# A transformer block on one core: who scales and copies the first tiles, eighteen extra turns of the identity, and the order in which the convolution's first operands are made

## What is computed

```python
def _layernorm(x, axis=-1, eps=1e-05):
    m = jnp.mean(x, axis=axis, keepdims=True)
    v = jnp.var(x, axis=axis, keepdims=True)
    return (x - m) / jnp.sqrt(v + eps)
...
        x = lax.conv_general_dilated(inputs, conv_w, window_strides=(1,), padding='SAME', dimension_numbers=('NWC', 'WIO', 'NWC')) + conv_b
        q, k, v = jnp.split(x, 3, axis=-1)
...
        scores = jnp.where(causal, scores, NEG_INF)
        p = jax.nn.softmax(scores, axis=-1)
        o = jnp.einsum('bhqk,bkhe->bqhe', p, vh)
        o = jnp.einsum('bqhe,hed->bqd', o, wo) + bo
        o = o.reshape(N, L, W_)
        return o @ proj_w + proj_b
...
    x = x + _L0_attn_ref(_layernorm(x, axis=-1), ...)
    x = x + _L0_ffn_ref(_layernorm(x, axis=-1), ...)
```

## Time and profile before

| | |
|---|---|
| median of 3 runs | 822.52 us (820.74 to 822.99) |
| the profiled execution | 821.56 us, of which the span of instructions is 819.7 us |
| TensorE busy, share of the span | 790.8 us, 96% |
| VectorE busy | 463.6 us, 57% |
| ScalarE busy | 407.5 us, 50% |
| GpSimd busy | 196.7 us, 24% |
| mean granted clock of TensorE | 0.997 |

### The profile page before, as it was taken

One profiled execution on the slowest core, in us unless ns is written; L12 is line 12 of the kernel. 1 busy time (PEld: TensorE's weight loads), 2 busy tenths in 40 slices (PEclk: granted clock), 3 DMA queues, 4 the chain that ended last, 5 costly groups with the idle time before them and its releaser, 6 DMA issues.

```text
span 819.7 us, 14315 instructions
## 1 busy us (share of the span) xinstructions
PE 790.8 (96%) x5248; PEld 704.1 (86%) x5248; DVE 463.6 (57%) x1359; ACT 407.5 (50%) x1085; POOL 196.7 (24%) x184
## 2 busy tenths in 40 slices
PE   3899999999999999999999999999999999999997
PEld 3798887777778788888888888888789999999996
DVE  6899966778877643333333434444684444444441
ACT  5953342344335997676868686867750111111010
POOL 2300103223230434252525253432300010100000
PEclk9999999999999999999999999999999999999999
DMA  8745833533436221211252411202143231313201
GB/s 333 254 123 173 261 121 114 205 120 110 155 141 239 88 106 39 105 39 72 94 235 84 114 62 49 90 1 104 67 139 108 75 104 52 103 52 103 73 31 52
DMA packets 41369, 94.03 MB, mean 115 GB/s; under 512 B 9299, under 2 KB 18387, under 8 KB 40020
## 3 DMA queue, kind: packets, MB, share of 16 engines
q1 hardware_dynamic: 38996, 84.73, 31.0%
q0 software_dynamic: 2304, 8.39, 2.5%
HBM read 66.63 MB, written 26.08 MB: 113 GB/s over the span
## 4 chain that ended last, share of the span: by engine, by line
PE 78%; DVE 11%; ACT 5%; issue 3%; POOL 2%; DMA 0%; DVEq 0%; ACTq 0%; POOLq 0%
PE net_psum L63 15%; PE net_psum L65 15%; PE net_psum L64 15%; PE net_psum L1208 10%; PE net_psum L1275 5%; PE net_psum L1294 4%; PE net_psum L1286 4%; POOL raw L478 2%; PE net_psum L1192 2%; PE net_psum L1326 2%; PE net_psum L1327 2%; PE net_psum L1340 2%; PE net_psum L1328 2%; DVE raw L891 1%; DVE raw L892 1%
## 5 line engine op out<-in xcount | busy, mean ns | idle before, releaser
L63 PE MATMUL net_psum<-fw_hi,xT_hi 128*128 128x354 f32 (+1 forms) x384 | 126.0, 328 | 0.4 <-DVE fw_lo L1059 0.4
L65 PE MATMUL net_psum<-fw_hi,xT_lo 128*128 128x354 f32 (+1 forms) x384 | 124.4, 324 | 0.0
L64 PE MATMUL net_psum<-fw_lo,xT_hi 128*128 128x354 f32 (+1 forms) x384 | 124.2, 324 | 0.0
L495 POOL TENSOR_TENSOR pr<-pr,rrec 128x512 f32<-128x512 f32 x64 | 66.7, 1042 | 219.9 <-DVE rrec L958 213.5
L631 ACT ACTIVATE pr<-pr,negmax 128x128 f32<-128x128 f32 x256 | 99.2, 392 | 12.3 <-DVE negmax L965 12.3
L1208 PE MATMUL net_psum<-ua,wa 128*128 128x256 f32 x384 | 85.5, 385 | 2.3 <-DVE ua L849 2.3
L1208 PEld LDWEIGHTS net_psum<-ua,wa 128*128 128x128 f32 x384 | 73.7, 193 | 12.7 <-issue 2.6
L965 DVE CUSTOM_DVE_ANT_0 pr<-net_psum,mask 128x128 f32<-128x128 f32 x256 | 58.8, 287 | 42.6 <-PE net_psum L1275 42.5
L63 PE MATMUL net_psum<-x_hi,w_hi 128*128 128x512 f32 x192 | 77.1, 401 | 3.2 <-DVE w_lo L898 3.0
L63 PE MATMUL net_psum<-c_hi,wqk_hi 128*128 128x256 f32 x256 | 76.8, 300 | 0.4 <-ACT kf L640 0.4
L478 POOL TENSOR_TENSOR raw<-raw 128x512 f32<-128x512 f32 x24 | 37.3, 1557 | 164.5 <-ACT raw L578 164.5
(11 more groups left out here) (174 smaller groups left out, 1824.0 us busy)
## 6 DMA issues: line engine op xcount, KB each, us to landing
wa<-in_conv_w SPq DMA_DIRECT2D x24, 512.0 KB, 4.1
raw<-in_conv_w SPq DMA_DIRECT2D x24, 384.0 KB, 3.4
xn<-in_x SPq DMA_DIRECT2D x16, 512.0 KB, 10.1
xr<-in_x SPq DMA_DIRECT2D x8, 1024.0 KB, 5.0
x_scratch<-xr SPq DMA_DIRECT2D x8, 1024.0 KB, 4.0
x1t<-x_scratch SPq DMA_DIRECT2D x16, 512.0 KB, 4.0
out<-y POOLq DMA_DIRECT2D x16, 512.0 KB, 5.0
c_raw<-c_scratch SPq DMA_DIRECT2D x7, 768.0 KB, 4.7
```

Of the source, the lines that this page charges most:

```text
L63: pe.matmul(out, w_hi, x_hi, start=first, stop=False)
L64: pe.matmul(out, w_hi, x_lo, start=False, stop=False)
L65: return pe.matmul(out, w_lo, x_hi, start=False, stop=last)
L495: pool.tensor_tensor(pr[:, jj % 4], pr[:, jj % 4], rrec[:, jj % 4].unsqueeze(2).to_broadcast([P, UN, P]), ALU.mult).then_inc(s["p_ready"], 1)
```

## The change

In the front three things change. ScalarE and VectorE trade work: VectorE scales tiles 5, 6 and 7 of sequence 0 (before: 2, 6, 7), copies the whole turned tile 6 and half of tile 7 (before: half of tile 7), and brings the statistics of the first tile to an end before it begins those of the second. TensorE gets 18 products of the identity with itself (`FILL`), behind the turns of sequence 0 and ahead of the first unit; their result is not used. At the start of the split units, steps are moved: on ScalarE `high_weight(1)`, `pre_scale(2)` and the last `high_input` go ahead of the last `first_out`; on VectorE `low_weight(0)` goes behind the last `inputs` and `low_input(6)`.

The change's own description also names a reordering from attention to dense in the tail. No line of the diff is in that part, and the instructions of GpSimd and SyncE stand in the same order in both kernels.

```diff
-    DVE_SCALES = (2, LT - 2, LT - 1)
+    DVE_SCALES = (LT - 3, LT - 2, LT - 1)
+    ACT_OUT = LT - 1
...
+    FILL = 18
...
             def conv_slot(k):
-                if k + 1 < NK:
+                if 0 < k < NK - 1:
                     high_weight(k + 1)
-                if k == 0:
-                    high_input(DC - 1)
                 if k % NP4 == 0 and k:
                     evacuate(k // NP4 - 1)
-                if k + 2 < NK:
+                if 0 < k < NK - 2:
                     pre_scale(k + 2)
...
-            for j in range(LT):
+            for j in range(LT - 1):
                 if j not in DVE_SCALES:
                     scale(0, j)
                 if j:
...
             high_weight(0)
             first_out(4)
             high_input(6)
+            high_weight(1)
+            pre_scale(2)
+            high_input(7)
             first_out(5)
...
-                for j in range(lo, LT):
+                for h in range(2):
+                    half_statistics(n, lo, h)
+                moments(n, lo)
+                add_eps(n, lo)
+                for j in range(lo + 1, LT):
                     half_statistics(n, j, 0)
-                    if j > lo:
+                    if j > lo + 1:
                         moments(n, j - 1)
+                    if j != lo + 2:
+                        finish(n, max(j - 2, lo))
+                    half_statistics(n, j, 1)
                     if j > lo + 1:
-                        finish(n, j - 2)
-                    half_statistics(n, j, 1)
-                    if j > lo:
                         add_eps(n, j - 1)
...
-                if k == 0:
-                    low_input(DC - 1)
...
+            dve.wait_ge(s["transposed"], LT - 1)
+            planes = stepped(xT, 32 * (LT - 2), (N * ROW, DC), (QUADS + 1, 4), (1, 32))
+            dve.tensor_copy(planes, turned(0, LT - 2).rearrange("p b (c t k) -> p (b c) k t", k=4, t=32)).then_inc(s["xT_dve"], 1)
...
-                if c == DC - 2:
-                    low_weight(0)
+            low_weight(0)
+            low_input(DC - 1)
...
             for j in range(LT):
                 transpose_tile(0, j)
+            pe.wait_ge(s["xT_ready"], LT // 2 + 1)
+            for i in range(FILL):
+
+                pe.transpose(turned(0, LT // 2)[:, 0, i % 4 * P:(i % 4 + 1) * P], ident[:], ident[:])
             for a in range(NA):
```

More of the change, by code:

```diff
@@ L1113, in _ @@
             dve.tensor_copy(planes, turned(0, LT - 1)[:, 1].rearrange("p (c t k) -> p c k t", k=4, t=32)).then_inc(s["xT_dve"], 1)
-            dve.wait_ge(s["xT_ready"], LT)
+            dve.wait_ge(s["xT_ready"], ACT_OUT)
+            dve.wait_ge(s["xT_dve"], 1)
             first_inputs(0, 0, 1)
             first_inputs(0, 1, 1)
-            dve.wait_ge(s["xT_dve"], 1)
+            dve.wait_ge(s["xT_dve"], 2)
             for c in range(2, DC, 2):
@@ L1123, in _ @@
                 inputs_of(0, c, c + 1)
-            dve.wait_ge(s["xT_ready"], N * LT)
+            dve.wait_ge(s["xT_ready"], ACT_OUT + LT)
             for c in range(0, DC, 2):
@@ L1189, in transpose_tile @@
                 normalised(n, j)
-                wait(pe, s["xT_ready"], j - 3 if n == 0 else LT + j - 1)
+                wait(pe, s["xT_ready"], j - 3 if n == 0 else ACT_OUT + j - 1)
                 for c in range(DC):
@@ L1200, in first_unit @@
                     if d == 0:
-                        pe.wait_ge(s["xT_ready"], LT)
-                        pe.wait_ge(s["xT_dve"], 1)
+                        pe.wait_ge(s["xT_ready"], ACT_OUT)
+                        pe.wait_ge(s["xT_dve"], 2)
                     wait(pe, s["a_evac"], 2 * (d - 1))
```

## The result

| | before | after |
|---|---|---|
| median of five runs each, side by side | 821.51 us (820.74 to 822.99) | 817.11 us (816.88 to 817.28) |
| the profiled execution | 821.56 us, span 819.7 | 817.15 us, span 815.4 |
| TensorE busy in it | 790.8 us | 791.7 us |
| mean granted clock in it | 0.997 | 0.999 |

The ratio is 0.9944 (95% interval 0.9932 to 0.9956): 4.4 us faster, inside the range and 0.8 under the predicted time. The two profiled executions lie 4.41 apart.

What follows compares the result with a forecast made beforehand. TensorE, busy 96% of the span, was taken as the bound. Gains 1.0 + 1.9 - 0.85 + 0.67 + 0.98 + 0.5 = 4.2 us gave 817.4 or 818.3, middle 817.9; range 816.0 to 820.3.

Steps and rivals of the forecast that it cites:

- The front: Sequence 0 ahead of the first unit: that unit starts at 24.85 instead of 25.83, gain 1.0 us (0.5 to 1.3).
- The two new costs on VectorE: In the front: uncovered aggregate of tile 0, 0.3 us, and the whole copy of tile 6, 1.3 us.
- ScalarE's last scale: In the front: now tile 4, expected near 17.3 to 18.5 us; TensorE's last four tiles were reckoned from 18.5.
- The late rise of the clock: Rival, turns of sequence 0: low clock lasts through their small pauses; 821.5, or 819.5 to 820.5 if risen before 25; chance 0.10.
- The clock: First 48 unit products: the 18 products close the empty stretch and the clock stays at 1.00, gain 1.9 us or 0.
- main case: Whole kernel: all terms hold, gain 4.2 us, time 816.3 to 819.2; chance 0.62.
- the clock falls all the same: Rival, first units: 1.9 lost but unit 0's 0.85 wait goes; gain 3.1, 818.5 to 819.4 us; chance 0.16.
- The split units: First split units: new wait of 0.85 us at unit 0, against waits of 0.67, 0.98 and 0.5 of 0.57 won.
- the overlap: Ahead of the split units: GpSimd's `mix(2)` runs inside VectorE's `inputs(7)`, costing VectorE 1.1 us.
- The half of 0.96 added for the median: Final time: median of runs stood 0.96 above the profiled execution, so the middle of 817.4 and 818.3 was taken.
- Gain given back later: Rival, behind the changed places: for instance a transfer due by the clock takes it back; 821.6 to 822.5 us; chance 0.04.
- VectorE no earlier: Rival, long stretch before the split units: VectorE gains nothing, unit 0 waits 2.85; 819.4 to 820.3 us; chance 0.08.

Runs made afterwards that it cites:

- the order alone: The kernel before with only the moved steps on ScalarE and VectorE at the first split units: 819.07 us, ratio 0.9971 (12 runs).

## Why the prediction was right, and where it was off

**The bound** was read rightly: TensorE is busy 97% of the span, and what was won at the two places is still won at the end.

**The front** was worth 0.79 by the profiles, not 1.0. The two new costs on VectorE were 0.34 and 1.23, as the working had them (0.3 and 1.3). What it had too early is ScalarE's last scale: TensorE turns the last four tiles from 18.80, not from 18.5, and VectorE waited 0.30 for tile 6. Another 0.17 is the start of the first statistics, 5.83 instead of 5.66 in this pair of executions. The quicker copy, and 2.15 instead of 2.24 from the half copy to the first unit, gave part of this back. The late rise of the clock, a rival, did happen in a small way: 8 turns took 1.67 at 16.75, where 16 in 1.75 is the full rate. It was over before the last four tiles.

**The clock.** The products took 0.109 us each, as predicted, ended 0.48 ahead of the first unit, and the clock stayed at 1.00: 1.69 won in the 48 products, against 1.9 predicted. The working set three times 3.46 against 12.29, but 48 in a row at the higher level take 10.60, not 10.38. The page of the Trainium skill that the prediction weighed, "TensorE: Matmul & The Clock Gate", Part 4 (PE-mode transpose), says that a transpose does not count as PE work in the same way and that the full rate does not engage for it. By it the products would hold nothing. The traces disagree: the clock read 1.00 behind them in all six profiles, and was low in six of eight without them.

The step that failed is the one ahead of it: "Now the first 48 unit products took 12.29 ... so 48 would take 10.38: 1.9 us were lost after the empty stretch". This took one execution's low stretch for a property of the kernel. By the mean clocks five of 50 executions have none, and 18 have two. Alone the products are worth 0.84 in the medians: by the mean clocks a part of the executions keeps a low stretch that they don't reach. In the changed kernel they are worth 0.86 in the medians (817.97 to 817.11), or 0.95 against the executions with a low stretch, because there a TensorE that is not slowed meets unit 0's wait; with that wait gone it is 1.62. The working foresaw this second mechanism: its main case and its rival "the clock falls all the same", 4.2 and 3.1, put 1.1 there.

**The split units.** VectorE began `inputs(7)` at 106.29 (106.1 predicted), lost 1.06 to the overlap (1.1), and TensorE waited 0.68 for unit 0 (0.85). The recorded waits 0.67, 0.98 and 0.57 went, and the last two stayed (0.84 in all, 0.8 predicted). The terms were mis-sized by one thing: a wait costs more than its record. The last first units and unit 0's first product, before and, as the third row, the last first units in the change:

```profile
107.11 10.52 PE L1208 MATMUL net_psum<-ua,wa 128*128 128x256 f32 x48
117.28 0.58 PE L63 MATMUL net_psum<-x_hi,w_hi 128*128 128x512 f32 x1
...
112.83 2.32 PE L1217 MATMUL net_psum<-ua,wa 128*128 128x256 f32 x10
```

Before, unit 0's first product began at 117.28, that is 0.35 ahead of the recorded end of the last first unit; after, it waits for 0.68 from that end, so the new wait costs 1.03. Taking it away was worth 0.95 in the medians. Likewise units 1 and 2 gain 0.92 and 1.24 where 0.67 and 0.98 were written in the rows. A short hold leaves no record at all, as at unit 0 in the order alone (0.28). Unit 7 gains 0.44 (0.5 predicted): it starts 5.89 behind unit 6, where 5.60 is usual, at 155.42, right behind the end of its `low_weight` at 155.37.

**The sum.** 0.79 + 1.69 - 1.03 + 0.92 + 1.24 + 0.44 is 4.05, a further 0.09 lies between units 2 and 3, and the rest of the 4.41 is spread over the 650 us behind. The working had 4.2. The front and the clock brought 0.42 less than it had and the split units 0.27 more, so that the sum came this close is partly luck. Taken from the profiled execution it gave 817.4, 0.3 from the result. The half of 0.96 added for the median was an error: the 822.52 of three runs was an accident of which low stretches they had, and the median over the 50 executions is 821.62, close to the profiled execution's 821.56.

**"Gain given back later"** didn't happen. **"VectorE no earlier"** fell with the 106.29.

## What to carry to other kernels

Before a term of a sum is taken from a stretch at a low clock, look at the clock in several executions: whether it falls behind a short empty stretch can differ from one execution to the next, and filling the stretch then buys a steadier time as much as a shorter one. Work of GpSimd that nobody waits for yet should not be released while VectorE makes an operand that TensorE waits for; here putting one `pre_scale` behind a copy was worth 0.95 us. A recorded wait of TensorE is a lower bound: here three of them cost 0.25 to 0.35 us more than their rows say. Two gains that end in the same wait are not independent: time how much lateness the next wait takes up before pricing either.

## What the runs showed of the hardware

- The granted clock fell behind an empty stretch of 2.4 us in six of eight profiled executions without the products, and stayed at 1.00 in two. What decides it was not found: the clock had risen at 14.7 to 18.1 us where it fell, and at 14.6 and 17.5 where it didn't. A second fall, among the last turns, was seen in one execution, behind pauses of 1.36, 0.94 and 0.99 us; pauses of 1.20, 0.94 and 0.98 in one other and of 1.32, 0.94 and 0.99 in a third, with the products, had none behind them. A mean clock of 0.995 or less, which went with two low stretches, stands in 21 of 62 executions with the turns of before (the kernel before and the order alone) and in one of 24 with the new turns and no products. So the changed front, whose pauses are 0.21 and 0.38 at 16.75 and 18.80, seems to be rid of that second fall; this is argued from the mean clocks, no profile shows it by itself.
- In the overlaps of GpSimd and VectorE seen here the one that began later paid. In the changed kernel `mix(2)` began at 110.34, VectorE's piece at 110.68, and the piece took 1.06 longer; with 36 products the overlap fell on the `low_input` at 111.52 behind a `mix(2)` that began at 111.34, and that took 3.37 instead of 2.28. With `pre_scale(2)` put behind the copy, `low_weight(1)` began at 116.59, 0.11 ahead of `mix(2)`; it kept its 1.22, and `mix(2)` took 2.26, ending 1.15 behind it. (The 1.72 of `mix` in the next two units is no undisturbed time either: each began inside a `low_weight` and ended 1.14 behind it.) The Trainium skill, "SBUF — State Buffer", "Who interferes with whom", says so: a VectorE instruction with two inputs in SBUF contends with a GpSimd instruction that reads SBUF for a port pair that only one of them can have, and the order of issue decides which of the two is blocked. These three overlaps agree.
